# Half-width edge products in a graph layer: 35 edge chunks a step, 45 products in alternating column halves

## The chip, the cores and the metric

One NeuronCore of a Trainium2 chip runs the whole layer in one launch. The metric is the device time of that launch in microseconds (us). The engines are PE (TensorE; its weight loads are shown apart as PEld), DVE (VectorE), ACT (ScalarE), POOL (GpSimd) and SP (SyncE, which issues DMAs).

## What is computed

12,500 nodes of 256 features and 212,500 edges, sorted by target node, all float32. After a layer norm (`xn`), each node gets three things: a graph sum with a two-layer perceptron, a hyperbolic attention mix, and a feed-forward part for the better half of the nodes. Cut to what matters:

```
msgs = edge_val[:, None] * x[edge_src]
agg = jax.ops.segment_sum(msgs, edge_dst, num_segments=N)
support = (1.0 + eps) * x + agg
h = jax.nn.relu(support @ W1.T + b1)
return h @ W2.T + b2
...
xn = _layernorm(x, axis=-1)
x = x + _L0_gnn_ref(xn, edge_weight, ...) + _L0_mix_ref(xn[None], ...)[0]
x = x + _L0_ffn_ref(_layernorm(x, axis=-1)[None], ...)[0]
```

The change is in how `agg` is summed.

## The kernel before

Nodes stand in 98 tiles of 128, and a *step* handles two tiles (49 steps, index `i`). A prologue normalises all nodes, writes `xn` to memory and finds, for each tile, where its edges begin (`tables_*`). Then the steps run, software-pipelined: step `i` does the edge sum of its 256 nodes and the mix of the same nodes (`mix_*`), and beside them the tail of step `j = i-1` (`tail_*`: the perceptron, second norm, output) and the feed-forward part of an older pair `m` (`ffn_*`). The feed-forward part runs in 42 of the 49 steps (`FFN_AT`: from 2 on, all but each ninth) and its last seven pairs after the loop.

**The edge sum.** The edges of a tile are cut into chunks of 128 (a *slot*; 18 a tile, 36 a step). For each slot POOL gathers 128 rows of `xn` into one of 18 message buffers (`msg`, L781; the ring's pace is the semaphore `slot_used`), DVE builds a 128x128 selection matrix from target and weight of each edge (`sel`, L975), and PE multiplies: `agg[h] += sel.T @ msg` (L1170), a float32 product with 256 moving columns, which the trace shows as two passes, each with its weight load. POOL may be up to 18 slots ahead of PE, DVE up to 12 (`SEL_RING`), and the DVE program builds the matrix of slot `k+8` at slot `k` (`LEAD`). When a step's last product is in, DVE takes the sum out (`take_sup`, L1033).

**The order of the other work** is written by hand: each engine's program walks over the slots `k` of a step, and the tables `PE_AT` and `DVE_AT` name the slot behind which each other piece stands. On PE these are: `mix_qkv` (L1193 transposes, L1194 products; half 0 ahead of slot 0, half 1 behind slot 10), `tail_supT` (L1222), `ffn_turn` (L1251), `tail_w1` (L1230), `tail_w2` (L1239), `mix_h1` (L1184, three), `mix_outT` (L1204, two), `mix_ft` (L1214, two), `ffn_hidden` (L1265, four) and `ffn_project` (L1277, four). On DVE, `combine` (L1043 to L1048) needs PE's `tail_w2`; then `mix_recip`, `mix_ratio`, `mix_om` (L988 to L1000) make `om`, which PE's `mix_outT` turns. ACT ends its use of the `qkv` banks for a half at L817 (`v_read`), for which PE's next `mix_qkv` waits.

Each engine runs its own list in order and waits on semaphores. The rare tile with more edges than its slots has a loop for the rest (`remainder`, `rem_chunk`); on the inputs used here it is never entered, in either kernel.

## Time and profile before

| | |
|---|---|
| runs (3) | median 2581.78 us, 2580.93 to 2582.52 |
| profiled execution, its own time | 2585.47 us |
| its span, first to last instruction | 2583.9 us |
| granted PE clock, mean over the span | 0.986 of full |
| busy share of the span | PE 96%, PEld 83%, DVE 69%, POOL 66%, ACT 55% |
| the steps, first to last `take_sup` | 215.5 to 2454.7 us, 48 steps |

The profile is of one execution. It lists groups of instructions by line with count, busy time and mean length, the idle time ahead of them and what ended it. Matmuls overlap in the engine's pipeline, so their lengths (380 ns) are more than their spacing; the chain of work that ended last shows the spacing. A few words of names: `bank` and `qkv` are PSUM banks, `rings` holds `msg` and `sel`, `work` is scratch, `resident` the transposed nodes.

### The profile page before, as it was taken

The page shows a single profiled execution, that of the slowest core. Times are in us where ns is not written, and L with a number is a line of the kernel's source. Part 1 is how long each engine was busy: PE and PEld are TensorE (multiplying, and loading weights), DVE is VectorE, ACT ScalarE, POOL GpSimd, SP SyncE. Part 2 cuts the span into 40 slices and gives each one's busy share as a digit, 9 for nine tenths or more (in the row PEclk, how much of TensorE's full clock was granted, in tenths as well). Part 3 has the DMA queues.
Part 4 walks back from the last instruction along what each step waited for, and adds up shares of the span by engine and source line. Part 5 has one row for each costly group of instructions (what it writes and reads, how often), then busy time and mean ns, then how long its engine had stood idle before and what let it go on. Part 6 is the DMA issues. An engine that isn't in the chain of part 4 may idle for free.

```text
span 2583.9 us, 41907 instructions
## 1 busy us (share of the span) xinstructions
PE 2472.5 (96%) x12655; PEld 2151.3 (83%) x12655; DVE 1794.8 (69%) x5939; ACT 1430.8 (55%) x3219; POOL 1712.5 (66%) x1881
## 2 busy tenths in 40 slices
PE   4789999999999999999999999999999999999996
PEld 4777888888888888888888888888888888888786
DVE  8847776776767768677677676776867767767567
ACT  3545665656656556466565664655646656556431
POOL 1247777777777777777777777777777777777400
PEclk9889999999999999999999999999999999999998
DMA  6734444344443444443434444344444343443338
GB/s 206 256 110 123 121 122 127 115 118 127 119 130 112 119 119 118 128 121 117 121 114 119 127 118 130 112 118 120 118 126 123 115 125 113 118 127 118 89 118 283
DMA packets 192003, 333.42 MB, mean 129 GB/s; under 512 B 46286, under 2 KB 133964, under 8 KB 191672
## 3 DMA queue, kind: packets, MB, share of 16 engines
q0 software_dynamic: 86752, 238.17, 31.6%
q1 hardware_dynamic: 105018, 92.42, 11.2%
q8 instruction: 113, 1.85, 0.3%
q14 instruction: 120, 0.98, 0.1%
HBM read 291.99 MB, written 38.46 MB: 128 GB/s over the span
## 4 chain that ended last, share of the span: by engine, by line
PE 86%; DVE 8%; DMA 3%; ACT 2%; issue 1%; SPq 0%; DVEq 0%
PE bank L1170 26%; PE qkv L1265 13%; PE bank L1277 13%; PE bank L1184 10%; PE bank L1214 6%; PE qkv L1194 5%; PE bank L1239 3%; PE bank L1230 3%; PE qkv L1193 2%; PE bank L1204 2%; DMA work<-in_x 2%; DVE rings L975 1%; DMA xn_dram<-work 1%; DVE work L422 1%; DVE work L393 1%; PE bank L1251 1%
## 5 line engine op out<-in xcount | busy, mean ns | idle before, releaser
L781 POOL DMA_INDIRECT rings<-xn_dram,window x1764 | 1686.7, 956 | 643.7 <-issue 377.2
L1170 PE MATMUL bank<-rings 128*128 128x256 f32 x3528 | 884.6, 380 | 16.1 <-DVE rings L975 13.2
L1170 PEld LDWEIGHTS bank<-rings 128*128 128x128 f32 x3528 | 653.8, 190 | 105.3 <-DVE rings L975 22.1
L975 DVE TENSOR_SCALAR rings<-iota,window_dst,window 128x128 f32<-128x128 f32 x1764 | 560.1, 358 | 160.8 <-PE bank L1170 138.8
L1265 PE MATMUL qkv<-work,ffn_weights 128*128 128x256 f32 x1568 | 365.5, 381 | 0.0
L1277 PE MATMUL bank<-ffn_weights,work 128*128 128x256 f32 x1568 | 362.0, 379 | 0.0
L871 ACT ACTIVATE work<-qkv,fb 128x256 f32<-128x256 f32 x392 | 160.1, 473 | 312.5 <-PE qkv L1265 312.0
L1277 PEld LDWEIGHTS bank<-ffn_weights,work 128*128 128x128 f32 x1568 | 297.2, 190 | 40.0
L1265 PEld LDWEIGHTS qkv<-work,ffn_weights 128*128 128x128 f32 x1568 | 295.7, 191 | 38.6
L1184 PE MATMUL bank<-resident,weights 128*128 128x256 f32 x1176 | 280.5, 382 | 0.0
L853 ACT ACTIVATE work<-bank 128x512 f32<-128x512 f32 x49 | 29.3, 597 | 403.2 <-PE bank L1222 403.2
L1184 PEld LDWEIGHTS bank<-resident,weights 128*128 128x128 f32 x1176 | 225.4, 192 | 31.1
L798 ACT ACTIVATE work<-qkv 128x1536 bf16<-128x1536 f32 x98 | 142.2, 1451 | 120.2 <-PE qkv L1194 120.2
L1194 PE MATMUL qkv<-weights,work 128*128 128x128 f32 x1176 | 202.6, 276 | 0.0
L1214 PE MATMUL bank<-weights,work 128*128 128x256 f32 x784 | 190.2, 386 | 0.1
L1194 PEld LDWEIGHTS qkv<-weights,work 128*128 128x128 f32 x1176 | 179.8, 193 | 3.6
L884 ACT ACTIVATE work<-bank,cols 128x256 f32<-128x256 f32 x294 | 150.1, 566 | 55.8 <-PE bank L1184 55.8
L1193 PE MATMUL qkv<-ident,work 128*128 128x128 f32 x588 | 161.9, 275 | 19.8 <-ACT work L817 18.5
L1214 PEld LDWEIGHTS bank<-weights,work 128*128 128x128 f32 x784 | 147.6, 192 | 28.9 <-ACT work L828 8.9
L1033 DVE SCALAR_TENSOR_TENSOR work<-work,cols,bank 128x512 f32<-128x512 f32 x49 | 36.6, 747 | 188.3 <-PE bank L1170 188.3
L1038 DVE TENSOR_TENSOR work<-work,b_row 128x512 f32<-128x512 f32 x49 | 34.3, 699 | 128.2 <-DMA work<-in_x 128.1
L317 ACT ACT_TABLE_LOAD x88 | 112.9, 1283 | 2.5 <-PEq L1606 0.9
(241 smaller groups left out, 3241.6 us busy)
## 6 DMA issues: line engine op xcount, KB each, us to landing
rings<-xn_dram,window POOLq DMA_INDIRECT x1764, 2.8
xn_dram<-work SPq DMA_DIRECT2D x14, 896.0 KB, 8.3
work<-xn_dram SPq DMA_DIRECT2D x49, 256.0 KB, 2.8
work<-in_x SPq DMA_DIRECT2D x48, 256.0 KB
out<-work SPq DMA_DIRECT2D x48, 256.0 KB
work<-in_x SPq DMA_DIRECT2D x7, 896.0 KB, 7.7
rings<-in_x SPq DMA_DIRECT2D x6, 896.0 KB, 9.4
rings<-out SPq DMA_DIRECT2D x6, 896.0 KB, 8.4
```

The source lines that it names most:

```text
L781: nc.gpsimd.indirect_dma_start(out=msg[q][:, :], out_offset=None, in_=xn_dram[:, :], in_offset=bass.IndirectOffsetOnAxis(ap=window[t % WIN ...
L798: s.activation(sq_dump, qkv.rearrange("p r i s c -> p (r i s c)"), ACT.Square, accum_out=nsq[h]).then_inc(nsq_ready, 1)
L871: ins = s.activation(hT[:, k], HID_BANK[q][:, e * D:(e + 1) * D], ACT.Gelu_apprx_tanh, bias=fb1[:, k:k + 1])
L884: ins = s.activation(h2T[:, k], H1_BANK[q][:, e * D:(e + 1) * D], ACT.Relu, scale=bn_a[:, k:k + 1], bias=bn_b[:, k:k + 1])
L975: v.tensor_scalar(sel[k % SEL_RING], iota[:, :], window_dst[b][:, k % SLOTS:k % SLOTS + 1], window[b][:, k % SLOTS, 2:3].bitcast(F32), ALU ...
L1170: te.matmul(agg[h], sel[k % SEL_RING], msg[q], start=first, stop=last, skip_group_check=True).then_inc(slot_used, 1)
L1184: ins = te.matmul(H1_BANK[q][:, e * D:(e + 1) * D], wqkvT[:, c, k * P:(k + 1) * P], h0T[:, c, 2 * i * P:2 * (i + 1) * P], start=(c == 0), ...
L1193: te.transpose(qkv[:, k // 2, k % 2, 0, :], lhs, ident[:, :])
L1194: ins = te.matmul(qkv[:, k // 2, k % 2, 1, :], lhs, mixW[:, k, :], start=True, stop=True)
L1214: ins = te.matmul(FT_BANK[h][:, 0:D], outT[:, c], wresT[:, c], start=(c == 0), stop=(c == 3))
L1265: ins = te.matmul(HID_BANK[q][:, e * D:(e + 1) * D], fw1[:, c, k * P:(k + 1) * P], x3T[:, c], start=(c == 0), stop=(c == C - 1))
L1277: ins = te.matmul(Y_BANK[:, h * D:(h + 1) * D], hT[:, k, h * P:(h + 1) * P], fw2[:, k], start=(k == 0 and h == 0), stop=(k == HC - 1), ski ...
```

## The change

**Chunks by step, not by tile.** A step's edges are now one run of 35 chunks, cut at the step's first edge. The 256 target nodes are seen as four quarters of 64; the edges of quarter q must lie in the chunks `QUARTERS[q]`, which overlap a little. A chunk that lies in one quarter's range alone is multiplied once, by a 128x64 selection matrix (64 columns of `sel`, 64 partitions of `agg`); a chunk in two ranges twice. That gives 45 half-width products a step for 36 full-width ones, 35 gathers for 36, and 45 DVE builds of 64 columns for 36 of 128. The products are listed so that they alternate between the left half of the PE columns (`agg[h][0:64]`) and the right one (`agg[h][64:128]`); in the built program they carry a tile size of 128x64, all other matmuls of the loop 128x128.

**Other work.** PE's step is written out, with `edges_to(n)` between the pieces; the DVE table is shifted to the 45 products. The last two `ffn_project` stand behind the last product, `tail_supT` and `ffn_turn` ahead of the first. `LEAD` is 12, `SEL_RING` 22, and the edge lists of a step come by seven DMAs into one of two buffers (before: one DMA a tile into one of four).

**Tables.** The prologue finds the first edge of each quarter, tests on the device whether the targets are sorted (`tables_order`, two DVE passes over 128x1664, and one more load of the targets), and works out from it which chunks beyond the ranges are needed (`tables_extra`, some 60 DVE instructions of one partition, behind the last norm group). Another piece of the diff, not shown, is the loop for extra chunks, which isn't entered here, and one semaphore for each buffer of the last copy in place of one for each copy.

```diff
-SEL_RING = 12
-LEAD = 8
+SEL_RING = 22
+LEAD = 12
 EARLY_EDGES = 12
-WINDOWS = 4
+WINDOWS = 2
+SLOTS = 35
+BLOCKS = (0, 7, 10, 15, 19, 24, 27, 35)
+QUARTERS = ((0, 10), (7, 19), (15, 27), (24, 35))
+LEFT = ((0, 1, 2, 3, 4, 5, 6, 7, 8, 9), (15, 16, 17, 18, 19, 20, 21, 22, 23, 24, 25, 26))
+RIGHT = ((10, 11, 12, 13, 14, 7, 8, 9, 15, 16, 17, 18), (27, 28, 29, 30, 31, 32, 33, 34, 24, 25, 26))
...
+def products():
+
+
+    order = []
+    for h in range(2):
+        for left, right in itertools.zip_longest(LEFT[h], RIGHT[h]):
+            order += [(2 * h + side, k) for side, k in enumerate((left, right)) if k is not None]
+    return order
+
+
+PRODUCTS = products()
...
+GATHERS = list(dict.fromkeys(k for _, k in PRODUCTS))
...
+FREED = [max(LAST_USE[k] for k in GATHERS[:n + 1]) for n in range(SLOTS)]
...
-        rings = sb("rings", [P, RING * D + SEL_RING * P])
+        rings = sb("rings", [P, RING * D + SEL_RING * P // 2])
         msg = [rings[:, D * q:D * (q + 1)] for q in range(RING)]
-        sel = [rings[:, RING * D + P * q:RING * D + P * (q + 1)] for q in range(SEL_RING)]
+        H = P // 2
+        sel = [rings[:, RING * D + H * q:RING * D + H * (q + 1)] for q in range(SEL_RING)]
...
+        def tables_order(dve):
+            v = nc.vector
+            dve.wait_ge(next_landed, 16)
+            v.tensor_tensor(rows, rows, rows_next.bitcast(I32), ALU.is_gt).then_inc(order_compared, 1)
+            dve.wait_ge(order_compared, 1)
+            v.tensor_reduce(unsorted_col, rows.rearrange("p c j -> p (c j)"), AX_X, ALU.max).then_inc(order_ready, 1)
...
+        def tables_extra(dve):
+
+
+            v = nc.vector
+            at_row = lambda n, w: marks[:, n * NS:(n + w) * NS]
...
                     stats(g + 2)
+            tables_extra(dve)
...
-        PE_AT = dict(sup=0, x3=0, qkv=10, w1=1, h1=(12, 17, 20), w2=4, outT=(13, 23), ft=(16, 27), hid=(23, 23,
-                     27, 29), y=(31, 32, 32, 35))
-        DVE_AT = dict(scale=(5, 10), out=(6, 13), c=(12, 18), ft=(14, 29), sup=0, n4=1, f=4, y=5, x=3,
-                      combine=(6, 12), rstd=16, tail_out=(20, 24), stage=(0, 27))
+        PE_AT = dict(w1=2, w2=6, qkv=12, h1=(16, 22, 25), outT=(18, 28), ft=(20, 32), hid=35, y=(38, 41))
+        DVE_AT = dict(scale=(6, 12), out=(8, 16), c=(15, 22), ft=(17, 36), sup=0, n4=1, f=5, y=6, x=4,
+                      combine=(7, 15), rstd=20, tail_out=(25, 30), stage=30)
...
+        def load_window(eng, i):
+            first = eng.value_load(bounds[0:1, 4 * i:4 * i + 1], min_val=0, max_val=ET * P)
+            if i >= WINDOWS:
+                eng.wait_ge(slot_used, RING + (i - WINDOWS + 1) * STEP_PRODUCTS)
+            for k0, k1 in zip(BLOCKS, BLOCKS[1:]):
+                eng.dma_start(window[i % WINDOWS][:, k0:k1, :].rearrange("p k c -> p (k c)"),
+                              edges[bass.ds(first * 3 + 3 * P * k0, 3 * P * (k1 - k0))].rearrange("(p n) -> p n", p=P)
+                              ).then_inc(window_landed[i % WINDOWS], 16)
...
+            for i in range(NS):
+                pool.wait_ge(window_landed[i % WINDOWS], WINDOW_DONE * (i // WINDOWS + 1))
...
+                for n, k in enumerate(GATHERS):
+                    G_ = i * SLOTS + n
+                    if G_ >= RING:
+                        back, m = divmod(G_ - RING, SLOTS)
+                        pool.wait_ge(slot_used, RING + back * STEP_PRODUCTS + FREED[m] + 1)
+                    else:
+                        pool.wait_ge(slot_used, RING)
                     nc.gpsimd.indirect_dma_start(
-                        out=msg[q][:, :], out_offset=None, in_=xn_dram[:, :],
-                        in_offset=bass.IndirectOffsetOnAxis(ap=window[t % WINDOWS][:, k, 0:1], axis=0)
...
+            def start_step(i):
+                b = i % WINDOWS
+                if i >= WINDOWS:
+                    dve.wait_ge(slot_used, RING + (i - WINDOWS + 1) * STEP_PRODUCTS)
+                dve.wait_ge(window_landed[b], WINDOW_DONE * (i // WINDOWS + 1))
+                v.tensor_scalar(window_dst[b][:, :], window[b][:, :, 1], float(-2 * P * i), None, ALU.add
                                 ).then_inc(dst_ready, 1)
 
...
+            def edge(i, n):
+                b, at_ = i % WINDOWS, i * STEP_PRODUCTS + n
+                q, k = PRODUCTS[n]
+                dve.wait_ge(slot_used, RING + max(0, at_ - SEL_RING + 1))
+                if n == 0:
+                    dve.wait_ge(dst_ready, i + 1)
+                v.tensor_scalar(sel[at_ % SEL_RING], iota[:, q * H:(q + 1) * H], window_dst[b][:, k:k + 1],
+                                window[b][:, k, 2:3].bitcast(F32), ALU.is_equal, ALU.mult).then_inc(sel_ready, 1)
 
...
+            def edge(i, n):
+                q, k = PRODUCTS[n]
...
+                h, side = q // 2, q % 2
+                first = h == 0 and n == FIRST_OF[q]
+                gathered = i * SLOTS + PLACE[k]
+                if n == 0:
                     after(pe, sup_ready, i)
-                if last:
-                    remainder(i, h)
-                pe.wait_ge(sel_ready, i * STEP_SLOTS + (k + 1))
-                pe.wait_ge(msg_landed[q], i * (16 * TURNS) + 16 * (k // RING + 1))
-                te.matmul(agg[h], sel[k % SEL_RING], msg[q], start=first, stop=last,
-                          skip_group_check=True).then_inc(slot_used, 1)
+                if n == STEP_PRODUCTS - 1:
+                    remainder(i, 0)
+                    remainder(i, 1)
+                pe.wait_ge(sel_ready, i * STEP_PRODUCTS + n + 1)
+                pe.wait_ge(msg_landed[gathered % RING], 16 * (gathered // RING + 1))
+                te.matmul(agg[h][side * H:(side + 1) * H], sel[(i * STEP_PRODUCTS + n) % SEL_RING], msg[gathered % RING],
+                          start=first, stop=n == STEP_PRODUCTS - 1, skip_group_check=True).then_inc(slot_used, 1)
...
+                    tail_supT(j)
+                if m is not None:
+                    ffn_turn(m, i)
+                edges_to(PE_AT["w1"])
+                if j >= 0:
+                    tail_w1(j)
+                edges_to(PE_AT["w2"])
+                if j >= 0:
+                    tail_w2(j, ran(i))
+                edges_to(PE_AT["qkv"])
+                mix_qkv(i, 1)
+                edges_to(PE_AT["h1"][0])
+                if i < NS - 1:
+                    mix_h1(i + 1, 0)
+                edges_to(PE_AT["outT"][0])
+                mix_outT(i, j, 0)
+                edges_to(PE_AT["ft"][0])
+                mix_ft(i, j, 0)
+                edges_to(PE_AT["h1"][1])
+                if i < NS - 1:
+                    mix_h1(i + 1, 1)
+                edges_to(PE_AT["h1"][2])
+                if i < NS - 1:
+                    mix_h1(i + 1, 2)
+                edges_to(PE_AT["outT"][1])
+                mix_outT(i, j, 1)
+                if m is not None:
+                    ffn_hidden(m, 0, i)
+                    ffn_hidden(m, 1, i)
+                edges_to(PE_AT["ft"][1])
+                mix_ft(i, j, 1)
+                if m is not None:
```

The order of instructions shows where this moves work. First PE, from the second `mix_outT` of a feed-forward step on (before: L1204 `mix_outT`, L1265 `ffn_hidden`, L1214 `mix_ft`, L1277 `ffn_project`, L1170 an edge product of two passes). Before:

```order
L1204 MATMUL bank<-ident,work 128x128 x4
L1265 MATMUL qkv<-work,ffn_weights 128x256 x8
L1170 MATMUL bank<-rings 128x256 x4
L1214 MATMUL bank<-weights,work 128x256 x4
L1265 MATMUL qkv<-work,ffn_weights 128x256 x4
L1170 MATMUL bank<-rings 128x256 x2
L1265 MATMUL qkv<-work,ffn_weights 128x256 x4
L1170 MATMUL bank<-rings 128x256 x2
L1277 MATMUL bank<-ffn_weights,work 128x256 x4
L1170 MATMUL bank<-rings 128x256
L1277 MATMUL bank<-ffn_weights,work 128x256 x8
L1170 MATMUL bank<-rings 128x256 x2
```

Behind these stand one more product and four L1277. The same stretch of the changed kernel (L1362, L1423, L1372, L1435 are the same pieces, L1328 is the half-width product):

```order
L1362 MATMUL bank<-ident,work 128x128 x4
L1423 MATMUL qkv<-work,ffn_weights 128x256 x8
L1328 MATMUL bank<-rings 64x256 x4
L1372 MATMUL bank<-weights,work 128x256 x4
L1423 MATMUL qkv<-work,ffn_weights 128x256 x4
L1328 MATMUL bank<-rings 64x256 x3
L1423 MATMUL qkv<-work,ffn_weights 128x256 x4
L1328 MATMUL bank<-rings 64x256 x3
L1435 MATMUL bank<-ffn_weights,work 128x256 x4
L1328 MATMUL bank<-rings 64x256 x3
L1435 MATMUL bank<-ffn_weights,work 128x256 x4
L1328 MATMUL bank<-rings 64x256 x3
```

Behind these stand one more product and eight L1435, so 17 half-width products in five groups have taken the place of 12 full ones in five. Second, PE behind `mix_qkv` half 0, up to `mix_qkv` half 1. Before (L1222 `tail_supT`, L1251 `ffn_turn`, L1230 `tail_w1`, L1239 `tail_w2`):

```order
L1170 MATMUL bank<-rings 128x256
L1222 MATMUL bank<-ident,work 128x128 x4
L1251 MATMUL bank<-ident,resident 128x128 x4
L1170 MATMUL bank<-rings 128x256
L1230 MATMUL bank<-work,weights 128x256 x4
L1170 MATMUL bank<-rings 128x256 x3
L1239 MATMUL bank<-weights,work 128x256 x4
L1170 MATMUL bank<-rings 128x256 x6
```

Changed:

```order
L1380 MATMUL bank<-ident,work 128x128 x4
L1409 MATMUL bank<-ident,resident 128x128 x4
L1328 MATMUL bank<-rings 64x256 x2
L1388 MATMUL bank<-work,weights 128x256 x4
L1328 MATMUL bank<-rings 64x256 x4
L1397 MATMUL bank<-weights,work 128x256 x4
L1328 MATMUL bank<-rings 64x256 x6
```

Five products ahead of `tail_w2` have become six half-width ones in two groups. Between that point and the second `mix_outT` stand 19 full products before and 22 half-width ones in seven groups now; a step has 14 such groups. Third, DVE from the first `combine` to the middle of the first `mix_om`, where only the builds (L975, now L1131) change in number and width. Before:

```order
L1043 TENSOR_TENSOR work<-work,bank 128x256
L1045 SCALAR_TENSOR_TENSOR work<-work 128x256
L1046 BN_STATS work<-work 128x6
L1048 BN_AGGR work<-work 128x2
L988 TENSOR_TENSOR bank<-bank,work 128x512
L989 TENSOR_TENSOR work<-work,bank 128x512
L975 TENSOR_SCALAR rings<-iota,window_dst,window 128x128
L994 SCALAR_TENSOR_TENSOR bank<-work,bank 128x512
L995 SCALAR_TENSOR_TENSOR bank<-work,bank 128x512
L975 TENSOR_SCALAR rings<-iota,window_dst,window 128x128
L998 TENSOR_REDUCE work<-work 128x16
L999 SCALAR_TENSOR_TENSOR bank<-work,bank 128x512
```

Changed:

```order
L1198 TENSOR_TENSOR work<-work,bank 128x256
L1200 SCALAR_TENSOR_TENSOR work<-work 128x256
L1201 BN_STATS work<-work 128x6
L1203 BN_AGGR work<-work 128x2
L1131 TENSOR_SCALAR rings<-iota,window_dst,window 128x64
L1143 TENSOR_TENSOR bank<-bank,work 128x512
L1144 TENSOR_TENSOR work<-work,bank 128x512
L1131 TENSOR_SCALAR rings<-iota,window_dst,window 128x64
L1149 SCALAR_TENSOR_TENSOR bank<-work,bank 128x512
L1150 SCALAR_TENSOR_TENSOR bank<-work,bank 128x512
L1131 TENSOR_SCALAR rings<-iota,window_dst,window 128x64
L1153 TENSOR_REDUCE work<-work 128x16
```

The builds stand closer together and are half as wide; from here to the second `om` (L1000, now L1155) DVE has 9 builds before and 11 now.

## Rows read from the trace of the kernel before

**Rows 1.** The page: busy time of each engine and the granted clock in 40 slices

```profile
PE 2472.5 (96%) x12655; PEld 2151.3 (83%) x12655; DVE 1794.8 (69%) x5939; ACT 1430.8 (55%) x3219; POOL 1712.5 (66%) x1881
...
PEclk9889999999999999999999999999999999999998
```

**Rows 2.** Groups by line: out<-in xcount | busy us, mean ns | idle before, releasers

```profile
L781 POOL DMA_INDIRECT rings<-xn_dram,window x1764 | 1686.7, 956 | 643.7 <-issue 377.2 <-PE bank L1170 216.3 <-PE bank L1315 50.2
L1170 PE MATMUL bank<-rings 128*128 128x256 f32 x3528 | 884.6, 380 | 16.1 <-DVE rings L975 13.2 <-DVE work L1033 2.0
```

**Rows 3.** The chain that ended last, one feed-forward step: start us, us, what

```profile
1295.73 2.59 PE bank L1170 x12
...
1300.10 0.22 PE qkv L1194 x2
1300.32 0.87 PE bank L1170 x4
...
1305.08 1.84 PE bank L1214 x8
...
1313.39 0.44 PE bank L1204 x4
...
1334.56 0.11 PE qkv L1193
1334.66 0.22 PE qkv L1194 x2
...
1336.55 0.43 PE bank L1170 x2
...
1338.29 1.81 PE bank L1230 x8
...
1341.41 1.99 PE bank L1239 x8
1343.40 2.59 PE bank L1170 x12
```

**Rows 4.** Timeline of DVE, L1033 (`take_sup`) at the ends of two kinds of step

```profile
1285.20 0.75 DVE L1033 SCALAR_TENSOR_TENSOR work<-work,cols,bank 128x512 f32<-128x512 f32 x1 [4.29 <-PE bank L1170]
1332.87 0.75 DVE L1033 SCALAR_TENSOR_TENSOR work<-work,cols,bank 128x512 f32<-128x512 f32 x1 [4.29 <-PE bank L1170]
1380.56 0.75 DVE L1033 SCALAR_TENSOR_TENSOR work<-work,cols,bank 128x512 f32<-128x512 f32 x1 [4.30 <-PE bank L1170]
1420.16 0.73 DVE L1033 SCALAR_TENSOR_TENSOR work<-work,cols,bank 128x512 f32<-128x512 f32 x1
```

**Rows 5.** The view of one line: L1033 and L781, durations ns, first and last start

```profile
L1033 DVE SCALAR_TENSOR_TENSOR work<-work,cols,bank x49: 734/748/749, 215.5 to 2454.7; 128x512 f32<-128x512 f32 x49
...
L781 POOL DMA_INDIRECT rings<-xn_dram,window x1764: 940/946/1464, 151.6 to 2430.9; - x196
```

**Rows 6.** Timeline of POOL, two gathers in a row

```profile
1305.70 0.95 POOL L781 DMA_INDIRECT rings<-xn_dram,window  x1 [0.30 <-issue]
1306.95 0.95 POOL L781 DMA_INDIRECT rings<-xn_dram,window  x1 [0.30 <-issue]
```

**Rows 7.** Timeline of DVE from `combine` past the second `om` of that step

```profile
1295.77 0.42 DVE L1043 TENSOR_TENSOR work<-work,bank 128x256 f32<-128x256 f32 x1 [1.64 <-PE bank L1239]
...
1300.54 0.35 DVE L975 TENSOR_SCALAR rings<-iota,window_dst,window 128x128 f32<-128x128 f32 x1
...
1312.42 0.69 DVE L1000 TENSOR_TENSOR work<-bank,work 128x512 f32<-128x512 f32 x1
...
1318.55 1.11 DVE L975 TENSOR_SCALAR rings<-iota,window_dst,window 128x128 f32<-128x128 f32 x4
```

**Rows 8.** Timeline of DVE in the prologue

```profile
16.03 1.89 DVE L258 TENSOR_REDUCE rings<-resident 128x13 f32<-128x1664 f32 x1
...
150.89 0.16 DVE L543 TENSOR_SCALAR work<-bank 128x1 f32<-128x1 f32 x1 [8.58 <-PE bank L511]
```

**Rows 9.** The chain in the prologue, the last two tiles of the norm and the early products

```profile
148.99 0.66 PE bank L503 x4
149.87 0.66 PE bank L503 x4
...
169.34 5.18 PE bank L1170 x24
```

More of the change, by code:

```diff
@@ L1 @@
+import itertools
 from contextlib import ExitStack
@@ L308, in tables_tensor @@
         def tables_tensor(pe):
             pe.wait_ge(ends_ready, 1)
-            for k in range(2):
-                nc.tensor.transpose(banks[k][0:EC, 0:P], ends[:, k, :], ident[:, :]).then_inc(ends_turned, 1)
+            nc.tensor.transpose(banks[0][0:EC, 0:P], ends, ident[:, :]).then_inc(ends_turned, 1)
         LN_EXP_SET, GELU_SET = 6, 11
@@ new lines, in rem_chunk @@
+                g.indirect_dma_start(out=rem_msg[:, :], out_offset=None, in_=xn_dram[:, :],
+                                     in_offset=bass.IndirectOffsetOnAxis(ap=rem_edges[:, 0:1], axis=0)
+                                     ).then_inc(rem_landed, 16)
+                for side in range(2):
+                    g.tensor_scalar(inside[:, side:side + 1], chunk, float(QUARTERS[2 * h + side][0]), BIG,
+                                    ALU.is_ge, ALU.mult)
+                g.tensor_scalar(dst_col, rem_edges[:, 1:2], float(-2 * P * i), None, ALU.add).then_inc(rem_dst_ready, 1)
@@ new lines, in rem_chunk @@
+                ins.then_inc(rem_dst_ready, 1)
+                counted(pool, rem_dst_ready, rem_turn)
+                for side in range(2):
+                    c0 = (2 * h + side) * H
+                    ins = g.tensor_scalar(rem_sel[:, side * H:(side + 1) * H], iota[:, c0:c0 + H],
+                                          inside[:, side:side + 1], rem_edges[:, 2:3].bitcast(F32),
+                                          ALU.is_equal, ALU.mult)
+                ins.then_inc(rem_ready, 1)
@@ L1068, in step @@
                 last = i == NS - 1
-                for k in range(STEP_SLOTS):
+                for k in range(STEP_PRODUCTS):
+                    if k == DVE_AT["stage"] and not last:
+                        start_step(i + 1)
                     ahead = k + LEAD
-                    nxt = ahead >= STEP_SLOTS
+                    nxt = ahead >= STEP_PRODUCTS
                     if not (last and nxt) and not (i == 0 and ahead < EARLY_EDGES):
-                        edge(i + nxt, ahead % STEP_SLOTS)
-                    if k == DVE_AT["stage"][0]:
-                        start_tile(2 * i + 1)
-                    if k == DVE_AT["stage"][1] and not last:
-                        start_tile(2 * i + 2)
+                        edge(i + nxt, ahead % STEP_PRODUCTS)
                     if j >= 0:
```

359 lines of the change are left out of this document (213 added, 146 removed).

## The prediction

> **What bounds the kernel now.** I read the page first: PE is busy 96% of the span at full clock, POOL and DVE about two thirds [rows 1]. That alone does not say that fewer PE passes help, so I went on to the chain that ended last. In a feed-forward step it is PE from end to end, without a hole, and such a step lasts 47.67 us from one `take_sup` (L1033) to the next [rows 4]. Twelve passes of the edge product take 2.59 us on it [rows 3], so one pass is spaced 0.216 us and one full product costs 0.432; 36 of them are 15.55 us of a step, the largest item by far. (The mean length of 380 ns in the groups [rows 2] is not the price: 164 ns of it is pipeline that overlaps the next pass.) A step without feed-forward lasts 39.60 us [rows 4]. From 215.5 to 2454.7 us there are 48 steps [rows 5], 46.65 us on average.
>
> Two other things stand close behind PE. POOL issues a gather each 1.25 us when nothing holds it [rows 6], 45.0 us for 36, and waits for PE only 216 us in all [rows 2]. And there is a chain on DVE: it sits idle until `tail_w2` ends, starts the first `combine` at 1295.77 and finishes the second `om` at 1313.11 (1312.42 and 0.69) [rows 7], 17.34 us later; PE begins to turn it at 1313.39 [rows 3]. So PE reaches its second `mix_outT` just when DVE is ready for it. PE work taken out between these two points comes back as a wait.
>
> **The change, part by part.** I cut a feed-forward step at these points: X, from the end of `mix_qkv` half 0 (1336.55) to the end of `tail_w2` (1343.40), 6.85 us; Y, from there to the second `mix_outT` (1295.73 to 1313.39), 17.66; Z, from it to the end of the next `mix_qkv` half 0 (1313.39 to 1336.55), 23.16 [rows 3]. They sum to 47.67.
>
> *Price of a half-width product.* It still moves 256 columns twice. No row shows one, so its price lies between two bounds. If nothing overlaps it is two passes, 0.432 us, like a full one. If the two column halves work side by side, the second pass of a left product runs with the first of the next right one, and a group of n alternating products takes n+1 pass times, (n+1) x 0.216. Even then the first and the last pass of each group are alone, and there are 14 groups a step. I take the lower bound, since neighbours share neither columns nor PSUM partitions, and name the upper one as a rival.
>
> The Trainium skill, "TensorEngine Tiling (Array Packing)", Key Properties, says that different tiles can run weight loads and matmuls in parallel, and "TensorE: Matmul & The Clock Gate", Part 3, gives 2.38 times for three column tiles; no row here shows it. By them the price would be near the lower bound.
>
> - X: 5 full products (2.16 us) become 6 half ones in 2 groups, 8 passes, 1.73: -0.43.
> - Y: 19 full (8.21) become 22 in 7 groups, 29 passes, 6.26: PE's work falls by 1.94 to 15.7. But DVE's 17.34 stay. DVE's builds follow each other at 0.253 us ((1.11 - 0.35)/3 in a run of four); a column costs 0.9 ns (512 columns of L1000 take 0.69, 128 of a build 0.35) [rows 7], so 64 fewer make it 0.195. 9 builds of 2.28 become 11 of 2.15. Y falls by 0.1, and 1.8 us of slack opens on PE in it.
> - Z: 12 full (5.18) become 17 in 5 groups, 22 passes, 4.75: -0.43.
>
> Sum: -0.96 us a feed-forward step, though edge passes alone fell by 2.8.
>
> *Each change between 128x64 and 128x128 tiles.* No row has one. Lower bound 0: PE changes between transposes and products every 0.11 to 0.22 us in `mix_qkv` and loses nothing [rows 3]. Upper bound: the pipeline must empty, 164 ns, and the next weight load can't run ahead; a group whose load came late took 1.84 us (L1214) where eight passes are 1.73 [rows 3], 0.11 more; together 0.27. There are 28 changes a step, 4 in X, 14 in Y, 10 in Z; X and Z pay them in full, Y only beyond its slack. By kind the nearest row is the one that loses nothing; I take 0.02: 14 x 0.02 = +0.28.
>
> So -0.68 a feed-forward step, times 42: -29 us. The seven other steps have X and part of Y: -0.5 each, -4. The average step is then 46.0 us; POOL, with 35 gathers, needs 43.75 and does not bind. Its ring of 18 now also holds chunks that are used twice, some four at a time, which leaves about ten gathers, 12 us, of lead; no product waited for a landing before [rows 2]. Seven small edge-list DMAs on SP's queue in place of two come early in a step, behind the load of `xn` and ahead of the store of rows, for a buffer that POOL wants half a step later: cost 0, hidden by the running step's products; without that cover two or three us a step, the length of a landing. DVE's builds in all are 45 x 0.195 = 8.8 against 9.1: 0.
>
> *Prologue.* The order test adds two DVE passes of about 1.9 us over the targets and one reduction of 1.89 goes [rows 8]: +1.9. `tables_extra`, 60 instructions, 35 of them linked (about 0.2 us, the rest 0.08, an estimate: 9 us), falls into an idle of DVE of 8.58 us that ends at 150.89 [rows 8]. But it waits until all but seven tiles are through PE, and a tile takes 0.88 us [rows 9], so only the last 6.5 us cover it: +2.5. More bytes at the start: 0 to +4. Against it the twelve early products take 13 passes where 24 took 5.18 [rows 9]: -2.4. Together +2 to +6; I take +2.
>
> The sum is -31 us. On the profiled execution (2585.47, 1.57 above its span) that is 2554; its time stands 3.7 above the median of the runs, so the forecast is **2550 us**.
>
> **Rivals.**
>
> *The change of tile empties the array.* At 0.164 us each: X and Z +2.30, Y 2.30 less 1.8 of slack, +0.5, less 0.96: +1.8 a step, times 42: +77, 2659 us. At 0.27: 3.78 and 1.98, less 0.96: +4.8, +202, 2784. It decides at 0.96/14 = 0.07 us a change; above that the kernel is slower. For it speaks that a full-width pass needs both halves free; against it that changes of operation cost nothing.
>
> The Trainium skill, "TensorEngine Tiling (Array Packing)", Key Properties, states that "Changing tiling mode (not just tile) drains the TensorE". By that rule this rival holds; no trace here shows it.
>
> *No overlap.* 90 passes for 72: X +0.43, Z 34 for 24 passes, +2.16, Y 44 for 38, +1.30, PE again bounding it: +3.9 a step, +163: 2745 us. For it: the rows show only full-width passes, which never overlap. Against: disjoint columns and partitions.
>
> *The chains give way.* If DVE and ACT, fed sooner, finish sooner, the floor is POOL: 1715 gathers x 1.25 = 2144 us against 2279 from first to last gather [rows 5]: -135, 2447. Against it: Y is DVE's own work.
>
> **How the numbers follow.** Forecast (overlap, cheap changes, 2520 to 2577): 0.46. Dear changes of tile, 2577 to 2784: 0.36, of it 0.08 so near the turning point that no change is measured. No overlap: 0.12. Deeper gain, below 2520: 0.06 (by the chains, or by steps without feed-forward that gain more). A measurement of this kernel can tell 0.2%, 5 us. That gives faster 0.52 less 0.02 for a prologue that takes it back, 0.50; same 0.08; slower 0.42. The range reaches from 2520, below the forecast with free changes (2538), to 2735, which takes in the first rival's lower half and part of the second; outside are 0.06 below and 0.13 above. The forecast's own range is 2520 to 2577.
>
> **What would show it.** In the chain, six alternating products in a group should take about 1.5 us (2.59 before), and a group of full-width passes should start as they end; 0.1 to 0.3 us between them is the first rival. Feed-forward steps should be 47.0 us long, Y about 17.6 of it, with PE waiting for `om` (L1155) or for ACT by over 1 us a step. PE's busy time should fall, the gathers' waits for PE shrink. If a group of n takes 2n passes, the second rival holds. I am wrong at the root if six products take 2.6 us or feed-forward steps are over 48 us.

## The result and the profile after

The changed kernel takes 2651.74 us, median of 4 runs (2650.29 to 2652.74), the kernel before beside it 2581.36 us (2578.39 to 2582.52): ratio 1.0274, 95% interval 1.0256 to 1.0292, so 70 us slower. Its profiled execution took 2652.74 us with a span of 2651.0. The range on record holds it, but the forecast of 2550 had the kernel faster; the first rival, at 0.164 us a change of tile, had 2659.

The page of the changed kernel, busy time and the granted clock, beside [rows 1]:

```profile
PE 2470.1 (93%) x13536; PEld 1775.5 (67%) x13536; DVE 1848.6 (70%) x6385; ACT 1433.9 (54%) x3219; POOL 1668.7 (63%) x1834
...
PEclk9889999999999999999999999999999999999998
```

The row of the clock has the same tenths (mean over the span 0.982, before 0.986; 1.00 in the feed-forward step shown below), and PE is busy 2.4 us less in all. Its groups by line, where [rows 2] had the full-width product:

```profile
L936 POOL DMA_INDIRECT rings<-xn_dram,window x1715 | 1641.1, 957 | 753.6 <-issue 384.7 <-PE bank L1328 319.8 <-PE bank L1500 49.1
L1328 PE MATMUL bank<-rings 128*64 128x256 f32 x4410 | 700.8, 395 | 23.8 <-DVE rings L1131 21.9 <-DMA rings<-xn_dram,window 1.9
L1131 DVE TENSOR_SCALAR rings<-iota,window_dst,window 128x64 f32<-128x64 f32 x2205 | 610.5, 332 | 32.5 <-PE bank L1328 17.8 <-DVE work L1182 0.3 <-DVE work L1203 0.3
```

The edge products (L1328) fell from 884.6 to 700.8 us of busy time, although 4410 passes took the place of 3528, so half-width products overlap. Busy time merges overlapping records, so by itself it is not what a step saves. The gathers wait for PE 320 us, 104 more than before, although there are fewer of them. Products wait 22 us for builds and 1.9 for landings in the whole run; neither is the cause.

The view of `take_sup` and its timeline, beside [rows 5] and [rows 4]:

```profile
L1188 DVE SCALAR_TENSOR_TENSOR work<-work,cols,bank x49: 741/748/751, 223.2 to 2520.3; 128x512 f32<-128x512 f32 x49
```

```profile
1322.63 0.75 DVE L1188 SCALAR_TENSOR_TENSOR work<-work,cols,bank 128x512 f32<-128x512 f32 x1 [6.02 <-PE bank L1328]
1371.57 0.75 DVE L1188 SCALAR_TENSOR_TENSOR work<-work,cols,bank 128x512 f32<-128x512 f32 x1 [6.02 <-PE bank L1328]
1420.49 0.75 DVE L1188 SCALAR_TENSOR_TENSOR work<-work,cols,bank 128x512 f32<-128x512 f32 x1 [6.02 <-PE bank L1328]
```

A feed-forward step lasts 48.94 us (47.67 before), and DVE waits 6.02 us at its end for the last products (4.29 before). The first `take_sup` is 7.7 us later (223.2 against 215.5), the 48 steps to the last are 57.9 us longer (2297.1 against 2239.2), and 1.5 us come behind it. That is the 67 us between the two spans; the profiled execution of before stood some 4 us above its own median.

The chain that ended last, for one such step (start us, us, what), beside [rows 3]:

```profile
1328.20 0.44 PE bank L1380 x4
...
1329.07 0.58 PE bank L1328 x4
1329.66 1.92 PE bank L1388 x8
1331.58 1.01 PE bank L1328 x8
...
1332.62 2.01 PE bank L1397 x8
...
1334.65 0.43 DVE work L1198
...
1344.15 1.97 PE bank L1372 x8
1346.11 1.01 PE bank L1328 x4
1347.12 1.92 PE bank L1342 x8
...
1351.97 1.01 PE bank L1328 x6
1352.98 0.59 PE bank L1362 x4
...
1371.50 3.65 PE bank L1435 x16
...
1377.14 0.44 PE bank L1380 x4
```

How to read it: each `L1328` entry is a group of edge products, two passes (x2) each. Two products take 0.58 us, four take 1.01, and three (x6) take 1.01 as well. So a left and a right product run side by side as a whole pair, 0.432 a pair; an odd one costs a pair too, and 0.15 is added at the start of each group. The full-width group behind takes 1.92 where its eight passes are 1.73: 0.19 more. The group of 1346.11 is the exception that explains the rest: its two products are both right ones (the list of the right side is two longer in the first tile), and one behind the other they take 1.01. With the prediction's cuts, X is now 6.43 us (1328.20 to 1334.63), Y 18.35 (to 1352.98), Z 24.16 (to 1377.14): -0.42, +0.69 and +1.00.

The boundary itself, the timeline of the matmuls and then of the weight loads:

```profile
1376.76 0.39 PE L1352 MATMUL qkv<-weights,work 128*128 128x128 f32 x2
1376.98 0.60 PE L1380 MATMUL bank<-ident,work 128*128 128x128 f32 x4
1377.42 0.60 PE L1409 MATMUL bank<-ident,resident 128*128 128x128 f32 x4
1377.95 0.65 PE L1328 MATMUL bank<-rings 128*64 128x256 f32 x4
1378.53 1.99 PE L1388 MATMUL bank<-work,weights 128*128 128x256 f32 x8
```

```profile
1376.87 0.47 PEld L1380 LDWEIGHTS bank<-ident,work 128*128 128x128 f32 x4
...
1377.95 0.20 PEld L1328 LDWEIGHTS bank<-rings 128*64 128x64 f32 x4 [0.17 <-issue]
1378.53 1.59 PEld L1388 LDWEIGHTS bank<-work,weights 128*128 128x128 f32 x8 [0.39 <-ACT work L1008]
```

Between full-width instructions the load runs ahead: that of L1380 starts at 1376.87, 0.11 ahead of its matmuls and under those of L1352. Across a change of tile the load starts together with the first matmul, in both directions (1377.95 and 1378.53), and that matmul starts only 0.07 before the modelled end of the other kind (1377.42 and 0.60; 1377.95 and 0.65), where L1409 starts 0.16 before the end of L1380. The releaser named at L1388, ACT L1008, is not what held it: that instruction had ended at 1378.22.

### The profile page after: what moved, and what is told of

Its sections match the earlier page's. It is cut to its first block, busy times and chain, and to the rows that moved or that the text cites. A ratio compares the mean times of both kernels' runs of the same rounds, so it can differ in the third digit from the quotient of the medians.

```text
span 2651.0 us, 44955 instructions
## 1 busy us (share of the span) xinstructions
PE 2470.1 (93%) x13536; PEld 1775.5 (67%) x13536; DVE 1848.6 (70%) x6385; ACT 1433.9 (54%) x3219; POOL 1668.7 (63%) x1834
## 3 DMA queue, kind: packets, MB, share of 16 engines
q1 hardware_dynamic: 140300, 92.36, 11.6%
## 4 chain that ended last, share of the span: by engine, by line
PE 70%; DVE 20%; ACT 4%; DMA 3%; issue 2%; SPq 0%; DVEq 0%
PE bank L1328 16%; PE qkv L1423 13%; PE bank L1435 12%; PE bank L1342 8%; PE bank L1372 7%; DVE rings L1131 4%; PE qkv L1352 3%; DMA work<-in_x 3%; PE bank L1388 2%; PE bank L1397 2%; PE qkv L1351 2%; PE bank L1362 1%; DVE work L525 1%; DVE work L496 1%; DVE work L1198 1%
## 5 line engine op out<-in xcount | busy, mean ns | idle before, releaser
L936 POOL DMA_INDIRECT rings<-xn_dram,window x1715 | 1641.1, 957 | 753.6 <-issue 384.7
L1328 PE MATMUL bank<-rings 128*64 128x256 f32 x4410 | 700.8, 395 | 23.8 <-DVE rings L1131 21.9
L1131 DVE TENSOR_SCALAR rings<-iota,window_dst,window 128x64 f32<-128x64 f32 x2205 | 610.5, 332 | 32.5 <-PE bank L1328 17.8
L1328 PEld LDWEIGHTS bank<-rings 128*64 128x64 f32 x4410 | 302.9, 136 | 313.0 <-issue 121.3
L1435 PE MATMUL bank<-ffn_weights,work 128*128 128x256 f32 x1568 | 375.1, 388 | 0.0
L1423 PE MATMUL qkv<-work,ffn_weights 128*128 128x256 f32 x1568 | 367.3, 382 | 0.0
L1435 PEld LDWEIGHTS bank<-ffn_weights,work 128*128 128x128 f32 x1568 | 286.8, 190 | 82.0 <-issue 32.3
L1423 PEld LDWEIGHTS qkv<-work,ffn_weights 128*128 128x128 f32 x1568 | 290.4, 190 | 51.8 <-ACT work L1026 16.1
L1342 PE MATMUL bank<-resident,weights 128*128 128x256 f32 x1176 | 295.3, 394 | 0.0
L1342 PEld LDWEIGHTS bank<-resident,weights 128*128 128x128 f32 x1176 | 213.2, 191 | 79.2 <-issue 55.7
L1008 ACT ACTIVATE work<-bank 128x512 f32<-128x512 f32 x49 | 29.3, 597 | 433.6 <-PE bank L1380 394.7
L1352 PE MATMUL qkv<-weights,work 128*128 128x128 f32 x1176 | 209.5, 282 | 0.0
L1372 PE MATMUL bank<-weights,work 128*128 128x256 f32 x784 | 195.7, 393 | 11.1 <-DVE work L1198 8.7
L1352 PEld LDWEIGHTS qkv<-weights,work 128*128 128x128 f32 x1176 | 186.8, 200 | 3.1
L1372 PEld LDWEIGHTS bank<-weights,work 128*128 128x128 f32 x784 | 141.6, 190 | 66.6 <-ACT work L983 34.9
L1351 PEld LDWEIGHTS qkv<-ident,work 128*128 128x128 f32 x588 | 86.5, 147 | 87.6 <-issue 85.0
```

The lines of the kernel that those rows point to most:

```text
L936: nc.gpsimd.indirect_dma_start(out=msg[G_ % RING][:, :], out_offset=None, in_=xn_dram[:, :], in_offset=bass.IndirectOffsetOnAxis(ap=window ...
L1131: v.tensor_scalar(sel[at_ % SEL_RING], iota[:, q * H:(q + 1) * H], window_dst[b][:, k:k + 1], window[b][:, k, 2:3].bitcast(F32), ALU.is_eq ...
L1328: te.matmul(agg[h][side * H:(side + 1) * H], sel[(i * STEP_PRODUCTS + n) % SEL_RING], msg[gathered % RING], start=first, stop=n == STEP_PR ...
L1342: ins = te.matmul(H1_BANK[q][:, e * D:(e + 1) * D], wqkvT[:, c, k * P:(k + 1) * P], h0T[:, c, 2 * i * P:2 * (i + 1) * P], start=(c == 0), ...
L1351: te.transpose(qkv[:, k // 2, k % 2, 0, :], lhs, ident[:, :])
L1352: ins = te.matmul(qkv[:, k // 2, k % 2, 1, :], lhs, mixW[:, k, :], start=True, stop=True)
```

## The experiments

### A full-width product written as two halves

`split_all` is the kernel before with one edit; `split_15` and `split_7` make it for the last product of each of its 15 places, or of 7 of them:

```
-  te.matmul(agg[h], sel[..], msg[q], ...).then_inc(slot_used, 1)
+  for side in range(2):
+      ins = te.matmul(agg[h][side * H:(side + 1) * H],
+                      sel[..][:, side * H:(side + 1) * H], msg[q], ...)
+  ins.then_inc(slot_used, 1)
```

> The kernel before, with each of the 36 edge products of a step issued as two half-width products (columns 0 to 63 and 64 to 127 of the same sel, same message block) one behind the other; nothing else differs, the builds, the places and the other engines' work are those of before. Places between full-width work: 15 a step. Theory A (each change between 128x64 and 128x128 tiles empties the array, 0.15 us going in and 0.19 us coming out, and the two halves of a pair run side by side): a pair lasts as long as one full-width product, 0.432, and a place costs 0.34, so +5.1 us of TensorE a feed-forward step, of which the slack between the two outT products hides a part: steps about 52.3 us, total about 2790 (range 2740 to 2830). Rival B (a half-width product costs like a full-width one, the halves do not overlap): +0.43 x 36 = +15.5 a step, about 3300. Rival C (the tiles cost nothing, the loss of the changed kernel came from its VectorE chain and prologue): 2582, as before.

> The kernel before, with only the last edge product of each of the 15 places of a step split into two half-width ones; 21 products stay full-width. Theory A (the price is one per change of tile size, whatever the number of half-width products between): the same as with all 36 split, about 2790, within 15 us of that run. Rival B (price per half-width product): 15/36 of that run's loss; if that run lost 210 us, this one loses about 88, 2670.

> As the run with 15 split products, but only at 7 of the places (products 4, 10, 16, 20, 27, 31, 35). Theory A: 7 places x 0.34 = 2.4 us a step, less what waits already cover: about 2670 (range 2650 to 2700). Rival B: 7/36 of the loss with all split, about 2620. If the loss were a fixed price of using both tile sizes at all in a step, this run would be as slow as that with 15.

Measured: `split_all` 2785.44 us (ratio 1.0784, 1.076 to 1.0809), `split_15` 2782.09 (1.0764, 1.0738 to 1.0791), `split_7` 2668.28 (1.0326, 1.03 to 1.0352). These kernels share data, builds, places and prologue with the kernel before. Fifteen split products cost what 36 do, so the price is per change of tile, and none is on the half-width product. Seven places cost 85 us, fifteen 199, per place 12 and 13 us of the whole run. A feed-forward step is 49.66 us with seven and 52.22 with fifteen, for 47.67: 0.28 and 0.30 a place, a little under the price in the chain, since some places stand at waits. The chain of `split_15`:

```profile
1362.85 0.86 PE bank L1176 x4
1363.72 0.58 PE bank L1173 x4
1364.30 0.59 PE bank L1210 x4
...
1370.22 1.92 PE bank L1220 x8
```

Two full products (L1176) take 0.86; the pair that does the work of one (L1173) takes 0.58, and the group behind it 0.59 for 0.44, or 1.92 for 1.73. That is 0.15 going in and 0.15 to 0.19 coming out, about 0.34 a place.

### The same products without alternation

`sides_apart` is the changed kernel, with all left products of a tile first:

```
-  for left, right in itertools.zip_longest(LEFT[h], RIGHT[h]):
-      order += [(2 * h + side, k) for side, k in enumerate((left, right)) if k is not None]
+  order += [(2 * h, k) for k in LEFT[h]] + [(2 * h + 1, k) for k in RIGHT[h]]
```

> The changed kernel, with the products of each tile in order of side, all left ones and then all right ones, in place of alternating; 45 products in the same 14 places. It computes the same. Theory A, by which two half-width products run side by side only when they follow one another in different halves: 45 x 0.432 = 19.4 us of products a step against some 25 x 0.432 = 10.8 in alternating order; +6 us a step after the waits that this covers, total about 2930 (range 2850 to 3030). Rival (halves never overlap, or overlap whatever the order): as the changed kernel, 2652.

Measured: 2897.01 us (ratio 1.1218, 1.1191 to 1.1246), 245 us above the changed kernel. The order of the gathers follows that of the products, but PE waits only 8 us between 400 and 2400, so the products themselves are what became longer. Its chain:

```profile
1375.10 1.44 PE bank L1327 x6
1376.54 1.92 PE bank L1434 x8
...
1381.83 1.87 PE bank L1327 x8
```

Three products of one side take 1.44 (3 x 0.432 and 0.15), four take 1.87, where alternating ones take 1.01. The overlap is real and depends on neighbours in different halves. Without it this change would have cost 314 us (against 2582.92 for the kernel before beside it).

### Fewer and fuller groups

`even_places` keeps 14 groups and evens their sizes; `eleven_places` merges some:

```
-  PE_AT = dict(w1=2, w2=6, qkv=12, h1=(16, 22, 25), outT=(18, 28), ft=(20, 32), hid=35, y=(38, 41))
+  PE_AT = dict(w1=2, w2=6, qkv=12, h1=(16, 22, 24), outT=(18, 28), ft=(20, 32), hid=36, y=(38, 42))   # even
+  PE_AT = dict(w1=2, w2=6, qkv=12, h1=(16, 20, 24), outT=(18, 28), ft=(20, 32), hid=38, y=(45, 45))   # eleven
```

> The changed kernel with the same 14 groups of products, their sizes 2, 4, 6, 4, 2, 2, 2, 2, 4, 4, 4, 2, 4, 3 (before 2, 4, 6, 4, 2, 2, 2, 3, 3, 4, 3, 3, 3, 4). Theory A with pairs (a group of n costs half of n, rounded up, times 0.432, and 0.34): 23 pairs in place of 25, 0.86 us less a step: about 2613 (range 2605 to 2630). If an odd product cost only half a pair, as the prediction's lower bound has it, nothing changes: 2652.

> The changed kernel with its other TensorE work in fewer places between the products: the places of PE_AT are 2, 6, 12, 16, 18, 20, 20, 24, 28, 32, 38, 45, so 11 groups of products a step in place of 14, most of an even size. Nothing else changes, the same 45 half-width products alternate. Theory A (0.34 us for each group that stands between full-width work, and an odd product costs as much as a pair): 3 x 0.34 + up to 3 x 0.432 = 1.0 to 2.3 us less a step, some 1.6 after waits: about 2580 (range 2560 to 2610). Rival (the loss sits in VectorE's chain between the outT products): no gain, or slower where the products come late, 2650 to 2700.

Measured: `even_places` 2615.66 us (ratio 1.0125, 1.011 to 1.0141), `eleven_places` 2582.61 (1.0002, 0.9993 to 1.0011). Evening alone is worth 36 us, 0.75 a step, so the pair as the unit is shown, and the prediction's n+1 passes, by which nothing would have changed, are refuted. (By the sizes a step has 26 pair times in the changed kernel and 24 in `even_places`; the expectation counted 25 and 23. The difference of two is what counts.) Three groups less, at the same 24 pair times, are worth another 33; 3 x 0.34 in 48 steps would be 49. By the chains of two feed-forward steps, 48.15 and 47.33 us long, the rest went to DVE: Z, with two groups less, is 0.63 shorter (23.75 to 23.12, for 0.68), but Y, with one less, only 0.18 (17.96 to 17.78), since in `eleven_places` the chain stays on DVE from the first `combine` to the second `om`. Chain of `even_places`, a group of four and one of two:

```profile
1343.20 1.01 PE bank L1328 x8
...
1346.14 0.58 PE bank L1328 x4
```

Then six groups, with left and right alternating through both tiles without a break, VectorE's order untouched (`six_places`) and moved (`six_places_dve`):

```
+  left = [(2 * h, k) for h in range(2) for k in LEFT[h]]
+  right = [(2 * h + 1, k) for h in range(2) for k in RIGHT[h]]
+  for pair in itertools.zip_longest(left, right): ...
+  PE_AT = dict(w1=0, w2=4, qkv=12, h1=(12, 20, 28), outT=(18, 28), ft=(20, 28), hid=28, y=(45, 45))
```

> The changed kernel with its other TensorE work at the places 0, 4, 12, 12, 18, 20, 20, 28, 28, 28, 28, 45, 45, so 6 groups of products a step (4, 8, 6, 2, 8, 17) in place of 14, and with left and right products alternating through both tiles of a step without a break, so 23 pairs. VectorE's order is that of the changed kernel. Theory A: 8 x 0.34 + 2 x 0.432 = 3.6 us of TensorE less a step, of which VectorE's chain leaves some 2.2 to 2.5: total about 2545 (range 2525 to 2575). Rival: beyond eleven groups the places bring nothing, since the other engines then wait for TensorE in long runs of products: 2580 or slower.

> The run six_places with VectorE's work of a step moved by a few places too (c 15, 22 to 19, 23; ft 17 to 16; f 5 to 6; y 6 to 5; combine 7, 15 to 8, 13; tail_out 25, 30 to 21, 32). If VectorE's chain between the two outT products bounds what is left, a step is a further 0.7 us shorter: total about 2515 (range 2500 to 2545). If TensorE alone bounds it, as six_places.

Measured: `six_places` 2547.97 us (ratio 0.9874, 0.9859 to 0.9889), 104 us faster than the changed kernel with the same 45 products. `six_places_dve` took 2526.55 (0.9781, 0.9768 to 0.9794), but in it the first tile's ft on DVE stands ahead of its factor c and uses that of an earlier step, so it leaves out a dependence of the layer, and its 21 us are not all a gain of order. The last run below takes that up.

### The prologue

`late_extra` and `late_extra2` move one call, with its scratch row and the reading of its counts; `no_order` drops the order test:

```
-            tables_extra(dve)                      # behind the norm
...
             early(6, EARLY_EDGES)
+            tables_extra(dve)                      # late_extra
             dve.wait_ge(stat_done, 1)
...
             v.tensor_tensor(bn_b, bet, t2, ALU.subtract).then_inc(bn_ready, 1)
+            tables_extra(dve)                      # late_extra2
```

> The changed kernel with tables_extra (some 50 small VectorE instructions, 11.3 us in the profile of the changed kernel, from 148.3 to 159.7) moved behind the statistics' products and the first twelve builds, where VectorE waits for TensorE; its scratch row and GpSimd's reading of the counts move with it. It computes the same. If the prologue's loss of 7.7 us (first take_sup at 223.2 against 215.5) is mostly this table standing on the path, the first take_sup comes 5 to 7 us earlier and the total is about 2646. If the loss is the order test and the waits for its transfers, nothing moves: 2652.

> The changed kernel without the test whether the edges are in order (no second load of the rows, no comparison and maximum over them, no transfer of the result; the flag is set to zero, which the data at hand would give). If the order test is on the path as its two VectorE instructions of 3.7 us are, the first take_sup comes 3 to 4 us earlier and the total is about 2648; if it is hidden, 2652.

> The changed kernel with tables_extra behind the whole of bn_vector, after bn_ready is given, so that neither TensorE's statistics' products nor the batch-norm factors wait for its 11 us (in the run late_extra the factors did, until 176, and TensorE then ran at 0.67 to 0.74 of its clock to 195). It computes the same. If the table on the path is what costs the prologue, the first take_sup comes 4 to 8 us earlier than 223.2 and the total is 2644 to 2648. If the first step's own chain on ScalarE and the lower clock after an idle stretch take it all back again, 2652 as before.

Measured: `late_extra` 2652.72 us (ratio 1.027, 1.0255 to 1.0284), no gain; `no_order` 2645.74 (1.0245, 1.0231 to 1.0258), 6 us; `late_extra2` 2645.28 (1.0244, 1.023 to 1.0258), 6 us. The timeline of DVE in the changed kernel has the table's first and last instruction and the statistics behind it:

```profile
148.32 0.06 DVE L366 MEMSET work<- 1x1 f32 x1 [2.25 <-PE bank L609]
...
159.62 0.19 DVE L409 CAST work<-work 1x98 int32<-1x98 f32 x1
159.74 0.14 DVE L649 TENSOR_SCALAR work<-bank 128x1 f32<-128x1 f32 x1
```

It stands for 11.4 us in front of statistics that began at 150.89 before [rows 8], and it costs more than that wait shows. Behind it PE had idled for 5.9 us, and its next sixteen passes ran in part at the lower clock (granted 0.68 on the mean from 156 to 165 us, 1.00 in `late_extra2`). The chains of the changed kernel and of `late_extra2`:

```profile
161.00 7.74 PE qkv L690 x16
```

```profile
155.77 5.16 PE qkv L690 x16
```

That is 5.2 us of start and 2.6 us of clock, 7.8 in all, of which 7.6 reach the first `take_sup` of `late_extra2`. With the table moved only one wait further (`late_extra`), the first `take_sup` is at 223.5, with it behind `bn_ready` at 215.6. What gave the first move back is in the chains of the changed kernel and of `late_extra`, and in the latter's windows (stretch and its length in us, busy time of PE, PEld, DVE, ACT and POOL, then the granted clock, the DMA share and GB/s):

```profile
183.94 1.85 PE bank L1342 x8
```

```profile
180.73 3.80 PE bank L1342 x8
```

```profile
180.00:190.00 10.00, 8.10 (x28) 6.46 (x27) 1.24 (x6) 2.85 (x7) 7.56 (x9) 0.50 0.43 131
```

In `late_extra` L690 starts at 156.13 and takes 5.18 us, so 7.4 us are won there. Then the table kept the batch-norm factors from PE, which was busy for 4.3 of the 10 us from 175 to 185, and the eight passes after that and `mix_qkv` behind them ran at half the clock, 1.2 GHz: 1.95 us more for L1342 alone. The 7.4 us were spent in the later factors and there.

The order test has two prices. Its load of the shifted rows goes out with the first loads of x; the chain's first entry in the changed kernel and in `no_order`:

```profile
1.44 13.52 DMA work<-in_x
```

```profile
1.44 10.36 DMA work<-in_x
```

3.2 us of transfer, and DVE's two passes. The first `take_sup` of `no_order` is at 216.0, with the table still in the path.

### Both together

> The run six_places with tables_extra where late_extra2 has it, and with five entries of VectorE's order moved: c of the second tile 22 to 23, ft of the first 17 to 16 (behind its c, at 15), combine 7, 15 to 8, 13, tail_out 25, 30 to 21, 32. It computes the same. (In six_places_dve c of the first tile stood at 19, behind the ft at 16 that uses it, so that this ft took the c of an earlier step.) If VectorE's order was worth something beside that misplaced c, a step is 0.2 us shorter than in six_places, 10 us in all, and the table gives 7 more as alone: about 2531 (range 2522 to 2545). If the 21 us between six_places and six_places_dve came only from the ft that did not wait for its c, the table's 7 remain: 2541.

Measured: 2532.41 us (ratio 0.9801, 0.9787 to 0.9814), 50 us faster than the kernel before beside it (2582.33) and 119 faster than the changed one. The medians lie 16 us below `six_places`, the two profiled executions 13. In these the 48 steps from the first `take_sup` to the last take 2180.3 us, 10 less than in `six_places` (2190.3); the table stands ahead of them, so that is the gain of VectorE's order. The first `take_sup` is 2.9 us earlier, by the table and that order together. `six_places_dve` has 2167.8. Its other 12 us came with the entries in which it differs, the c behind its ft and the places of f and y; no run separates them. A feed-forward step is 46.41 us. Its view of `take_sup`, and its chain:

```profile
L1189 DVE SCALAR_TENSOR_TENSOR work<-work,cols,bank x49: 737/748/749, 215.7 to 2395.9; 128x512 f32<-128x512 f32 x49
```

```profile
1273.13 0.43 DVE work L1199
...
1289.91 0.70 DVE work L1156
1290.65 0.65 PE bank L1363 x4
...
1299.94 4.04 PE bank L1329 x34
```

Seventeen products in one group take 4.04 us: nine pairs and one entry (9 x 0.432 + 0.15). Between the end of `tail_w2` and the second `mix_outT` the chain now stays on DVE, 17.48 us: that is the bound that the prediction gave to Y (17.34), and here it holds.

## Why the prediction was wrong

**The step that failed** is "each change between 128x64 and 128x128 tiles", priced at 0.02 us with bounds of 0 and 0.27. It measured about 0.15 in and 0.19 out, 0.34 for a pair of changes where the forecast had 0.04. The bounds were right, the choice between them was not. It went by the row "nearest in kind", the change between transposes and products in `mix_qkv`, which costs nothing; but those are both 128x128, so that row says nothing on tiles. The nearer evidence was what the upper bound was built from: a pass needs the whole array, and a late weight load costs 0.11. The rule of the Trainium skill, "TensorEngine Tiling (Array Packing)", Key Properties, that changing the tiling mode drains the engine, agrees with these runs: left and right tiles of one size follow each other freely, 128x64 and 128x128 do not. The prediction had it as a rival. Its own sign of being wrong at the root, a feed-forward step over 48 us, came true (48.94).

That the first rival's 2659 lies 7 us from the measured time is partly luck. Its price, 0.164 a change, is what was measured (0.17). But it had 1.8 us a feed-forward step, measured 1.27, and nothing for the other steps (+2.1) and the prologue (+7.7). The range held the time only by the part that was added for that rival.

**Price of a half-width product.** The direction was right (they overlap), the formula was not. A group that alternates costs half its size, rounded up, in pairs of 0.432, not n+1 passes. For six products that is 1.30 against the 1.51 forecast, and 1.45 with the 0.15 at its start. Summed over a step it is 26 x 0.432 = 11.2 us against the forecast's 59 passes, 12.7. With 14 x 0.34 = 4.8 for the changes it becomes 16.0, against 15.55 of before: the whole saving on PE went into the changes, and 0.4 more.

**X and Z.** X fell by 0.42, close to the forecast: `tail_w2` and `tail_w1` already took 1.99 and 1.81 for 1.73 of passes before [rows 3], so part of the way out stood under a wait that was there. Z was forecast at -0.23 and is +1.00: five groups of 3 or 4 products are 10 pairs and 5 places, 6.0 us, for 5.18 before, and `mix_outT` at its start pays 0.15 for the way out of Y's last group (0.59 for 0.44).

**Y.** Forecast about -0.1, measured +0.69. The timeline of DVE has both ends and a run of builds, as [rows 7] had, and that of PE has its two waits:

```profile
1334.65 0.42 DVE L1198 TENSOR_TENSOR work<-work,bank 128x256 f32<-128x256 f32 x1 [1.69 <-PE bank L1397]
...
1342.92 0.75 DVE L1131 TENSOR_SCALAR rings<-iota,window_dst,window 128x64 f32<-128x64 f32 x3
...
1351.69 0.69 DVE L1155 TENSOR_TENSOR work<-bank,work 128x512 f32<-128x512 f32 x1
```

```profile
1337.02 0.30 PE L1351 MATMUL qkv<-ident,work 128*128 128x128 f32 x1 [0.96 <-ACT work L972]
...
1344.15 1.97 PE L1372 MATMUL bank<-weights,work 128*128 128x256 f32 x8 [0.25 <-DVE work L1198]
```

From 1334.65 to 1352.38 are 17.73 us, 0.39 more than before: there are 11 builds for 9, and one is 0.22 us apart from the next ((0.75 - 0.31)/2), not 0.195. Halving the columns saved 0.03 of 0.253. But PE turns the second `om` only at 1352.98, 0.60 after DVE has it and not 0.28, so Y is not DVE's alone. DVE holds the chain up to its second `combine` (L1198), which frees the bank that `mix_ft` (L1372) writes; that part, from the end of `tail_w2` to `mix_ft`, is 9.52 us for 9.35. From there PE runs without a hole, 8.83 us for 8.31: three edge groups of 1.01 (0.43, 1.29 and 1.29 before) and three ways out of 0.13 to 0.19. The 1.8 us of slack that was to open on PE went to the changes: its products in Y cost 13 x 0.432 + 7 x 0.34 = 8.0 us for 8.21. What it waits there, 1.2 us a step, is mostly for ACT, which the forecast named among its signs but did not price.

**Steps without feed-forward** were to gain 0.5; the one that starts at 1420.49 takes 41.72 us against 39.60. By the chains 1.4 of the 2.1 us come before the end of `tail_w2`, where two `ffn_project` of the step before now stand behind `take_sup` (3.65 us for 1.73), and 0.6 in Y (18.31 for 17.71). Behind the second `mix_outT` DVE's builds hold the chain in both kernels, 11.8 us for 11.6.

**Prologue.** Forecast +2 (+2 to +6), measured +7.7. `tables_extra` was 11.4 us, not 9, and cost the path 5.2 us and, by the clock after PE's idle stretch, 2.6 more, where 2.5 were given to it and no clock; the bytes at the start cost 3.2, inside their range. The twelve early products cost 2.74 for 5.18, -2.4 as forecast. Taking away the order test or moving the table brings the first `take_sup` to 216, each alone. Whether the two add was not run.

**What held.** POOL does not bind, no product waited for a landing worth speaking of, and the small transfers on SP cost nothing seen. The second rival, no overlap, was 2745 and is refuted by `sides_apart`, which has that and lies 245 us above. The third did not occur in this kernel: POOL waited 320 us for PE, and Y grew.

## What to carry to other kernels

Half-width products pay in long runs that alternate between the halves: here a run had to save more than 0.34 us, so that fourteen short groups a step lost and six, one of them of seventeen products, won. Count the changes of tile size before counting passes, and when a row is to stand for an unknown cost, ask whether the thing priced (here the tile) changes in that row at all. Work on a small table in a prologue is worth placing twice: moved from one wait that PE had to another, it returned nothing. An idle stretch of PE is paid a second time in the clock behind it.

## What the runs showed of the hardware

- Two fp32 products of 128x64 tiles in different halves run side by side, both passes: 0.432 us for the pair, as for one full-width product (34 passes in 4.04 us). Neighbours in the same half do not overlap (four in 1.87).
- A change between 128x64 and 128x128 costs 0.15 us going in and 0.15 to 0.19 coming out, whatever stands between (2782 us with one split product in each of 15 places, 2785 with all 36 split). A weight load does not run ahead across it; it does between tiles of one size, 0.11 us and more. The Trainium skill, "TensorE: Matmul & The Clock Gate", Part 3, says in its list of what overlaps that a load overlaps matmuls in flight only when the row group differs, and above that list also when it goes to the background weight buffer. Here full-width loads, whose row groups are all the same, start under the matmuls of the line before (L1380 at 1376.87), so the row group alone does not decide; no row tells which buffer a load goes to.
- In a run of builds one of 64 columns starts 0.22 us behind the one before, one of 128 columns 0.253.
- After an idle stretch in the prologue PE ran at 1.2 GHz (granted 0.50 from 180 to 190 in `late_extra`), and eight passes took 3.80 us for 1.85.
